# Masked cross-attention in a two-layer perceiver block: value products in blocks of a pair of heads, and constants multiplied into unused banks at seven waits

## The reference

```python
qh = (q @ Wq.T).reshape(B, Sq, H, d).transpose(0, 2, 1, 3)
kh = (k @ Wk.T).reshape(B, -1, H, d).transpose(0, 2, 1, 3)
vh = (v @ Wv.T).reshape(B, -1, H, d).transpose(0, 2, 1, 3)
scores = jnp.einsum('bhqd,bhkd->bhqk', qh, kh)
scores = jnp.where(mask[:, None, :, :], jnp.float32(-1000000000.0), scores) * scale
attn = jax.nn.softmax(scores, axis=-1)
out = jnp.einsum('bhqk,bhkd->bhqd', attn, vh)
out = out.transpose(0, 2, 1, 3).reshape(B, Sq, Hd)
return out @ Wo.T
```

## Time and profile before

| | us |
|---|---|
| median of 3 runs | 1761.82 (1760.24 to 1762.29) |
| the profiled execution, its own time | 1760.35 |
| its span in the trace | 1758.9 |
| PE busy in it | 1684.7 |
| DVE busy in it | 1070.8 |
| ACT busy in it | 908.5 |

### The profile page before, as it was taken

The page is one execution under the profiler, slowest core; times in us unless marked ns, Lnnn a source line. Parts: engine busy times, 40 slices in busy tenths (PEclk is TensorE's granted clock), DMA queues, the critical chain, the costliest instruction groups (busy, mean ns, idle before and its releaser), DMA issues.

```text
span 1758.9 us, 29329 instructions
## 1 busy us (share of the span) xinstructions
PE 1684.7 (96%) x11102; PEld 1274.4 (72%) x11102; DVE 1070.8 (61%) x2282; ACT 908.5 (52%) x1910; POOL 126.1 (7%) x75
## 2 busy tenths in 40 slices
PE   7999999998999999999999999999999987999998
PEld 5778888886878788777777777756545555777776
DVE  5777777774643325555555555588744435787865
ACT  6666667562154224444444454477623334676763
POOL 0000000000000011000100010000011102223213
PEclk9999999998999999999999999999999997999999
DMA  6332323214620399777867786778760033888852
GB/s 234 116 108 84 96 85 96 85 60 174 239 96 0 114 287 323 228 236 216 238 190 232 220 239 185 209 197 227 256 242 7 7 132 124 285 307 288 285 194 75
DMA packets 147259, 308.53 MB, mean 175 GB/s; under 512 B 11453, under 2 KB 101565, under 8 KB 135549
## 3 DMA queue, kind: packets, MB, share of 16 engines
q1 hardware_dynamic: 145564, 301.65, 53.4%
q0 software_dynamic: 1536, 4.76, 0.9%
HBM read 225.16 MB, written 81.22 MB: 174 GB/s over the span
## 4 chain that ended last, share of the span: by engine, by line
PE 86%; DVE 5%; ACT 4%; issue 2%; DMA 1%; DVEq 1%; SPq 0%; POOL 0%; ACTq 0%; POOLq 0%
PE bank L128 16%; PE bank L130 14%; PE bank L129 14%; PE bank L1299 7%; PE bank L1321 5%; PE bank L1675 4%; PE bank L1289 3%; PE bank L2199 3%; PE bank L2203 2%; PE bank L2200 2%; PE bank L2234 2%; PE bank L1768 2%; PE bank L1332 2%; ACT T L1818 1%; DVE WS L2514 1%
## 5 line engine op out<-in xcount | busy, mean ns | idle before, releaser
L1418 DVE CUSTOM_DVE_ANT_0 TT<-bank,MASK 128x512 f32<-128x512 f32 x256 | 174.7, 683 | 22.5 <-PE bank L1289 21.8
L1365 ACT ACTIVATE TT<-TT,MX 128x512 f32<-128x512 f32 x256 | 183.5, 722 | 0.2
L2514 DVE TENSOR_TENSOR WS<-EW,WS 128x1024 fp32r<-128x1024 f32 (+1 forms) x120 | 146.9, 1234 | 59.2 <-ACT WS L2345 58.2
L2345 ACT CAST WS<-EW 128x1024 fp32r<-128x1024 f32 (+1 forms) x144 | 139.1, 977 | 50.4 <-PE bank L2203 48.7
L1299 PE MATMUL bank<-IDN,TT 128*128 128x128 f32 x1024 | 159.9, 279 | 0.0
L128 PE MATMUL bank<-BCH,WKT 128*128 128x256 f32 x512 | 154.6, 302 | 4.3 <-DVE BCL L355 4.3
L1431 DVE COPY PT<-bank 128x512 f32<-128x512 f32 x128 | 88.3, 690 | 102.1 <-PE bank L1299 99.3
L130 PE MATMUL bank<-BCH,WKT 128*128 128x256 f32 x512 | 145.3, 284 | 0.0
L129 PE MATMUL bank<-BCL,WKT 128*128 128x256 f32 x512 | 145.1, 283 | 0.0
L1299 PEld LDWEIGHTS bank<-IDN,TT 128*128 128x128 f32 x1024 | 116.0, 140 | 33.0 <-issue 22.2
L1373 ACT COPY PT<-bank 128x512 f32<-128x512 f32 x128 | 75.3, 588 | 113.1 <-PE bank L1299 113.0
(11 more groups left out here) (333 smaller groups left out, 3831.3 us busy)
## 6 DMA issues: line engine op xcount, KB each, us to landing
EW<-in_ewg SPq DMA_DIRECT2D x48, 1024.0 KB, 6.1
KST<-tmp_k SPq DMA_DIRECT2D x43, 768.0 KB, 5.7
tmp_k<-EKH SPq DMA_DIRECT2D x128, 256.0 KB, 2.8
EW<-in_ewg SPq DMA_DIRECT2D x24, 768.0 KB, 4.4
CT<-in_ctxT SPq DMA_DIRECT2D x32, 512.0 KB, 3.5
CN<-in_ctxN SPq DMA_DIRECT2D x32, 512.0 KB, 3.5
BCT<-in_ctxT SPq DMA_DIRECT2D x32, 512.0 KB, 4.4
tmp_k<-EKL SPq DMA_DIRECT2D x64, 256.0 KB, 2.8
```

What stands on the lines that cost most here:

```text
L1365: act.activation(TT[:, n % 4, cs], TT[:, n % 4, cs], ACT.Exp, bias=MX[:, n % 4, 5:6], scale=SC1, accum_out=SUM[:, b % 2, h, kc:kc + 1]).th ...
L1418: dve.tensor_tensor_reduce(TT[:, sl, 512 * kc:512 * kc + 512], bank[(0, 1, 4)[g % 3]][:], MASK[:, b % 2, 512 * kc:512 * kc + 512], 1.0, NE ...
L2345: act.copy(WS[:, i % NR, 0, 0:n * w], EW[q % NE][:, at:at + n * w]).then_inc(*w_high.up)
L2514: dve.tensor_tensor(WS[:, i % NR, 1, 0:n * w], EW[q % NE][:, at:at + n * w], f(WS[:, i % NR, 0, 0:n * w]), ALU.subtract).then_inc(*w_low.up)
```

## The change

There are three parts.

1. `value` is no longer issued for each unit but for eight at once: in unit g = 8p + 9 the values of parts 8p to 8p + 7 stand behind one another. The PT copies are kept until then, in 12 tiles in place of 4. Nothing else moves: turns, scores, projections and background steps keep their places, and so do the streams of the other engines; only the index in ACT's and DVE's waits for a free PT tile differs.
2. The sums are four matmuls with 32 weight columns in place of two with 64.
3. `keep_busy(n, bk)` issues n float32 matmuls of two constants, 128x128, into a bank that nobody uses then. They stand ahead of the seven waits, in the order of the program with n = 12, 14, 5, 12, 12, 8 and 9. They wait for nothing and nothing waits for them.

```diff
+        def keep_busy(n, bk):
+
+            for _ in range(n):
+                pe.matmul(bank[bk][:, 0:128], ONES[:], IDN[:], start=True, stop=True)
...
@@ finish @@
+                if b == 3:
+                    keep_busy(12, 4)
                 pe.wait_ge(*n_rows[4 + b])
                 rows_turned(b, 2).then_inc(*out_turn.up)
...
-        NP = 4
+        NP, NV = 12, 8
...
-                    for h in range(2):
-                        m = pe.matmul(bank[vb][64 * h:64 * h + 64, 256:384], ONES[:, 0:64], DG[:, h, :], start=True,
+                    for row in range(0, 128, 32):
+                        m = pe.matmul(bank[vb][row:row + 32, 256:384], ONES[:, 0:32], DG[:, row // 64, :], start=True,
                                       stop=True)
...
-                    value(g - 2)
+                    if (g - 2) % NV == NV - 1:
+                        for v in range(g - 1 - NV, g - 1):
+                            value(v)
...
@@ route @@
+                if b == 3:
+                    keep_busy(12, 0)
                 pe.wait_ge(*r_rows[b])
...
+                if b == 3:
+                    keep_busy(12, 0)
                 pe.wait_ge(*r_ind[b])
...
@@ attend @@
+                if b == 3:
+                    keep_busy(5, 1)
                 pe.wait_ge(*a_scaled[2 * b + 1])
...
+            keep_busy(14, 7)
             pe.wait_ge(*a_rows[0])
...
@@ experts_pe @@
+            keep_busy(8, 0)
             experts_open(pe)
             list_tokens(0, 0, 5)
...
             count = load_count(pe, 0)
+            keep_busy(9, 0)
             turn_zero(0)
```

## The result

| | before | after |
|---|---|---|
| median of 4 runs each, us | 1761.62 (1760.24 to 1762.29) | 1695.67 (1694.36 to 1700.95) |
| ratio, 95% interval | | 0.9632 [0.9610, 0.9654] |
| the profiled execution, its own time | 1760.35 | 1694.49 |
| its span | 1758.9 | 1693.2 |

The account below looks back on a forecast made before the run. PE was taken as the bound, with DVE taking over where no background work runs. 52 + 10 + 4.6 + 6.7 = 73.3 us off the profiled 1760.4 gave 1687.1, 1688 for the median, range 1677 to 1710.

Parts of the forecast that it names:

- The blocks with background work: Cross stage, pairs 0 to 19: PE stays the bound and each pair gets 2.6 us shorter, 52 us in all.
- DVE's wait for the sums: Cross stage with background work: DVE may sit idle about one unit, some 2.5 us, before each block; costed at nothing.
- lock-step: Rival, 17%: during a block DVE and ACT run dry and PE then waits for them; 1721, or 1698 in part.
- blocks that don't run together: Rival, 4%: PE empties itself at each wait inside a block, so little but the constants remains; about 1752.
- Without background work: Cross stage, pairs 20 to 29: DVE becomes the bound, so only 10 us are gained, bounds 0 and 12.
- a clock falling between blocks: Rival, 3%: without background work PE's clock goes to 1.2 GHz between blocks, making the kernel slower, 1768.
- DVE's floor of 9.45: Pairs without background work: DVE's own work is 9.45 us a pair, limiting the gain to at most 1.2 us.
- the 0.2 taken off for waits: Pairs without background work: 0.2 us a pair deducted from the gain for DVE's waits at a block's end.
- The constants: Float32 products at seven waits keep PE's clock from falling: 6.7 us gained, upper bound 12, lower a loss.
- the rival's mechanism: Rival, 12%: the clock falls in spite of the constants, each takes 0.45 us and delays the chain near 1460 us; 1698.
- the last two pairs, 4.6 us: End of the cross stage: no scores for DVE, so PE binds again and two pairs gain 2.3 us each.
- covered, by less than before: Cross stage without background work: keys land 5.7 us after issue and are asked for over 9 us ahead.

Follow-up runs that it names:

- e4_fours: The changed kernel with blocks of four values in place of eight, two blocks to a pair: 1701.25 us.
- e6_copy_to_act: The changed kernel with one of DVE's four copies of turned exponentials per pair made by ACT from unit 160 on: 1694.21 us.
- e11_short_copy: e9_fewer_loads with one of DVE's four copies per pair cut to 64 of 512 columns from unit 160 on, part of the output left out: 1689.09 us.
- e2_constants: The kernel before with only the constants added at the seven waits, values one by one and sums as before: 1754.93 us.
- e9_fewer_loads: The changed kernel with the next stages' loads one with every tenth unit in place of every fifth, from unit 200 on as before: 1694.33 us.
- e10_late_loads: The changed kernel with no loads for the next stages before unit 243, in place of 200: 1690.82 us.
- e5_early_loads: The changed kernel with the next stages' loads begun at unit 170 in place of 200: 1706.77 us.

## Why the prediction was right, and what it missed

**The blocks with background work** (forecast 52, measured 50.4): right in mechanism and nearly in size. An ordinary pair gave 2.45 us for the 2.61 of the sum. A lone value costs 0.55 us in an ordinary unit, not the 0.56 of the one place in the earlier trace rows, the unit with the sums gave back 0.82 us and not 0.56 + 0.37 = 0.93, and a block adds 2.28, not 2.24. Twenty times 2.45 are 49.0; the 50.4 of the column holds 1.4 us more because the block of the twentieth pair stands behind unit 160, so part of the closeness is where the column ends. By the Trainium skill, "TensorE: Matmul & The Clock Gate", on the per-tile semaphore tail, seven further increments of some 26 ns would be an estimated 0.18 us a block, 3.6 us in this part. These traces can't decide on it: a value in a block takes 0.23 us with its increment, 0.02 more than the 0.21 of the earlier trace rows, while the block as a whole adds only 0.04 us more than was priced, and no run takes the increments out.

**DVE's wait for the sums** cost nothing, as argued: 43.6 us of it, under PE's own work. So the lock-step did not come there, and the 72 records in 2.10 us rule out blocks that don't run together.

**Without background work** (forecast 10, bounds 0 and 12; measured 12.6, just past the upper one): the pair went to 9.40 us, as named in advance, and the clock stayed at 1.00, so that the rival of a clock falling between blocks did not come. DVE's floor of 9.45 from the earlier trace rows was 0.05 too high, and the 0.2 taken off for waits was not lost. That no engine but DVE stood near was too simple: by e4_fours, e6_copy_to_act and e11_short_copy another limit stands some 0.3 us behind it.

**The constants** (forecast 6.7): 6.2 us by e2_constants (3.9 to 8.5). That their columns agree with the forecast to 0.3 us in the one trace of the table is luck: up to unit 0, eleven traces with constants take 676.5 to 680.5 us and three without 680.4 to 681.3; in self-attention with the routing the table above shows a spread of 7 us. Over all these traces the means with and without constants differ by 2.3 and by 4.1 us, near the forecast's 2.8 and 3.9. Behind 420 us and behind the start of self-attention the clock stayed at 1.00. The first window of the earlier trace rows reads so in the changed kernel:

```profile
420.10:427.00 6.90, 6.09 (x17) 3.00 (x18) 4.08 (x5) 2.38 (x2) 0.00 (x0) 1.00 0.35 115
```

At the last place the rival's mechanism showed (0.47 us a constant, rows late), but the low stretch there was 10.2 us long for the 20.4 of the earlier trace rows, and the last two columns lost nothing in all.

**The step that failed: the last two pairs, 4.6 us, with the keys "covered, by less than before".** Two things were wrong in it.
- *The keys.* I set one landing time, 5.7 us from the earlier trace rows, against the lead of 9 us. That is a median over the whole kernel, at a share of 0.75 to 0.82. What the faster pace asks of the path was never worked out, though the earlier trace rows has the 228 GB/s of the old pace and the loads beside the keys stand in the code. The 0.82 is a mean, too: in the 30 us with weight loads the kernel before already stood at 1.01, with its keys landing in 6.8 to 7.8 us. In the changed kernel 312 GB/s were asked for there and 269 given, each load of keys landed later than the one before, and the last took 12.5 us. Cost: 5.3 us, by e9_fewer_loads and e10_late_loads.
- *The gain.* With keys in time the rest of the stage takes 23.9 us, 0.5 less than before and not 4.6. The timeline of the kernel before in its last pairs, two turns with a value between them:

```profile
1260.70 0.66 PE L1299 MATMUL bank<-IDN,TT 128*128 128x128 f32 x4
1261.28 0.42 PE L1321 MATMUL bank<-PT,VG 128*32 128x128 f32 x8
1261.64 0.66 PE L1299 MATMUL bank<-IDN,TT 128*128 128x128 f32 x4
```

Turn to turn it is 0.94 us, and in e9_fewer_loads two turns with nothing between them start 0.43 to 0.49 us apart, so a value here costs some 0.48 us, less than the 0.56 priced. In the changed kernel three blocks lie behind unit 240, since a block stands nine units behind the start of its pair: part of the gain credited to earlier units is work put off to here. And turns without values between them wait for the two banks that ACT and DVE empty; the timeline of PE in e9_fewer_loads:

```profile
1192.72 1.11 PE L1306 MATMUL bank<-IDN,TT 128*128 128x128 f32 x8 [0.33 <-ACT PT L1382]
...
1194.61 1.06 PE L1306 MATMUL bank<-IDN,TT 128*128 128x128 f32 x8 [0.78 <-ACT PT L1382]
...
1200.86 1.11 PE L1306 MATMUL bank<-IDN,TT 128*128 128x128 f32 x8 [0.33 <-ACT PT L1382]
```

An estimate from these numbers: a third block put off to here in place of two lone values 1.3 us (2.28 - 2 x 0.48), sixteen values at 0.48 for 0.56 another 1.3, and the three waits for banks 1.4. That is 4.0 of the 4.1 us that are missing, but no run tried the parts one by one.

**What stays open**: why the clock falls at about 1370 us in some executions and not in others of the same code, and whether the second point's three parts are each as large as estimated.

## What to carry to other kernels

Matmuls with few weight columns that alternate with full ones are worth gathering, as long as their operands can be kept: here 0.55 us became 0.23 for each group of four. When a stage gets faster, work out in GB/s what the new pace and all loads that run beside it ask of the transfers. A median landing time hid a path that was already full for 30 us; starting the prefetches earlier made it worse here, and thinning them out mended it. Price the last iterations of a pipelined loop by themselves, with what is put off into them, and constants that keep PE at work by the length of the wait at the clock that is granted there. Where two executions of the same code differ by 7 us in one stage, compare many of them before crediting an edit.

## What the runs showed of the hardware that I had not expected

- Keys, values and weights together got 245 GB/s through where the DMA engines' share was 1.03 (e5_early_loads), 269 and 284 where it was 1.01 (changed kernel, kernel before), while the loads behind 1370 us in e9_fewer_loads ran at 424 GB/s with a share of 1.02. So the same full share stood beside quite different GB/s in this case, and the share told better than the GB/s that the path was full.
- The granted clock fell at 1405.2 us in the changed kernel, just as a pause of 0.77 us began, behind 13.7 us in which PE was busy for 12.5, constants included. In e9_fewer_loads it fell at 1377.6 us, 2.3 us into products of 64 columns without a pause, ahead of which PE had stood still for 0.88 us. Neither fall stood behind a long pause.
